# Causal mask of single-head score banks: from a matmul into VectorE's row maximum

## What is computed

```python
scores = jnp.einsum('bhqd,bhkd->bhqk', q, k_h) / math.sqrt(HEAD_DIM)
causal = jnp.triu(jnp.ones((t, t), dtype=bool), k=1)
scores = jnp.where(causal[None, None], jnp.finfo(scores.dtype).min, scores)
attn = jax.nn.softmax(scores, axis=-1)
ctx = jnp.einsum('bhqk,bhkd->bhqd', attn, v_h)
return ctx @ Wo
```

## Time and profile before

| | us |
|---|---|
| three runs | 1482.33, 1478.23, 1481.91 |
| median | 1481.91 |
| the profiled execution | 1481.86 |
| its span | 1480.0 |
| TensorE, VectorE busy | 1381.3, 1026.3 |
| ScalarE, GpSimd busy | 729.4, 683.0 |

### The profile page before, as it was taken

How to read it: one execution, slowest core, us unless ns; L and a number is a source line. 1 busy time by engine, 2 the same in 40 slices (tenths; PEclk the granted TensorE clock), 3 DMA queues, 4 the chain that set the end, 5 groups by cost and what they waited for, 6 DMA issues and landing times. The chain is left out here.

```text
span 1480.0 us, 20324 instructions
## 1 busy us (share of the span) xinstructions
PE 1381.3 (93%) x7032; PEld 1085.2 (73%) x7032; DVE 1026.3 (69%) x1934; ACT 729.4 (49%) x1574; POOL 683.0 (46%) x533
## 2 busy tenths in 40 slices
PE   4779999988898699999999999999999999699999
PEld 3656666665676578888888888888888887578887
DVE  6768998785757587777877787777777787532323
ACT  3547887676434355454544444544544445243332
POOL 3448887666352544244333543434424431054543
PEclk9979999999999899999999999999999999899999
DMA  3000000100110211010110110101101010033332
GB/s 106 4 26 1 1 1 1 29 2 15 51 36 1 72 30 43 15 30 29 29 36 9 43 29 16 43 15 29 44 15 29 22 43 1 15 93 94 96 97 80
DMA packets 64933, 50.73 MB, mean 34 GB/s; under 512 B 5760, under 2 KB 54272, under 8 KB 64576
## 3 DMA queue, kind: packets, MB, share of 16 engines
q1 hardware_dynamic: 64832, 49.43, 11.7%
HBM read 47.32 MB, written 2.10 MB: 33 GB/s over the span
## 5 line engine op out<-in xcount | busy, mean ns | idle before, releaser
L1669 POOL TENSOR_TENSOR a_p_lo<-a_prob,a_p_hi 128x512 fp32r<-128x512 f32 x160 | 203.8, 1288 | 89.3 <-ACT a_p_hi L1559 87.2
L682 ACT ACTIVATE a_pt_hi<-a_ring 128x512 fp32r<-128x512 f32 x160 | 93.9, 596 | 172.0 <-PE a_ring L392 171.9
L818 POOL TENSOR_TENSOR a_rot_a<-a_rot_a,a_rot_b 128x512 f32<-128x512 f32 x80 | 103.4, 1293 | 151.1 <-DVE a_rot_b L561 150.3
L673 ACT ACTIVATE a_prob<-a_score,a_nmax 128x128 f32<-128x128 f32 (+3 forms) x256 | 132.2, 530 | 57.8 <-DVE a_nmax L526 57.7
L333 PE MATMUL a_xo<-h_hi,a_w_hi 128*128 128x512 f32 x384 | 154.0, 401 | 5.3 <-POOL a_w_lo L828 4.2
L2282 POOL TENSOR_TENSOR f_w_lo<-raw,f_w_hi 128x512 fp32r<-128x512 f32 (+2 forms) x66 | 90.5, 1395 | 145.2 <-ACT f_w_hi L2225 145.2
L335 PE MATMUL a_xo<-h_hi,a_w_lo 128*128 128x512 f32 x384 | 151.3, 394 | 0.0
L334 PE MATMUL a_xo<-h_lo,a_w_hi 128*128 128x512 f32 x384 | 150.1, 391 | 0.0
L823 POOL TENSOR_TENSOR a_p_lo<-a_rot_a,a_p_hi 128x512 fp32r<-128x512 f32 x80 | 103.6, 1295 | 70.3 <-ACT a_p_hi L699 70.3
L543 DVE TENSOR_TENSOR a_pt_lo<-a_ring,a_pt_hi 128x512 fp32r<-128x512 f32 x160 | 108.5, 686 | 32.6 <-ACT a_pt_hi L682 31.4
L1559 ACT ACTIVATE a_p_hi<-a_prob 128x512 fp32r<-128x512 f32 x160 | 99.7, 630 | 45.5 <-PE a_cbank L1190 43.2
(11 more groups left out here) (327 smaller groups left out, 3784.7 us busy)
## 6 DMA issues: line engine op xcount, KB each, us to landing
raw<-in_L_gate_up_t SPq DMA_DIRECT2D x40, 256.0 KB, 3.0
raw<-in_L_attn_wq SPq DMA_DIRECT2D x32, 256.0 KB, 2.9
raw<-in_L_attn_wo SPq DMA_DIRECT2D x32, 256.0 KB, 2.6
raw<-in_L_down_t SPq DMA_DIRECT2D x20, 256.0 KB, 2.7
x<-in_L_attn_x SPq DMA_DIRECT2D x4, 512.0 KB, 5.5
raw<-in_L_attn_wk SPq DMA_DIRECT2D x8, 256.0 KB, 2.8
raw<-in_L_attn_wv SPq DMA_DIRECT2D x8, 256.0 KB, 2.8
out<-x SPq DMA_DIRECT2D x8, 256.0 KB, 2.5
```

What stands on the lines that cost most here:

```text
L673: nc.scalar.activation(prob[i % 2][:, h, 0:n], score[e % NS][:, (h % per) * n:(h % per + 1) * n], ACT.Exp, bias=nmax[:, i % 2, h:h + 1], a ...
L818: nc.gpsimd.tensor_tensor(rot_a[:, c % 2, :], rot_a[:, c % 2, :], rot_b[:, c % 2, :], ALU.add).then_inc(summed, 1)
L1669: nc.gpsimd.tensor_tensor(p_lo[:, mm % NP, :], prob[:, mm % NE, :], p_hi[:, mm % NP, :].bitcast(F32), ALU.subtract).then_inc(p_ready, 1)
```

## The change

In banks of one head the mask matmul is gone, and the score matmul signals `scored` itself. VectorE reads the bank with `tensor_tensor_reduce`: it adds the bank and `mask_w`, scales by -1, writes that back to the bank (which nobody reads), and gives the minimum, which is the negated maximum of the masked row. Tiles 0 and 1 are as before, and so are the turned scores and the second attention.

```diff
+def masked_maximum(nc, m, bank, n, to):
+
+    scores = bank[:, 0:n]
+    return nc.vector.tensor_tensor_reduce(scores, scores, m.mask_w[:, T - n:T], -1.0, LARGE, ALU.add, ALU.min, to)
...
                 out = claim_score()
+                scored_by[QT * u + i] = count["score"]
+                if per == 1:
+                    nc.tensor.matmul(out[:, 0:n], q_rows[:, bank, :], k_rows[:, u % 2, x, 0:n], start=True,
+                                     stop=True).then_inc(scored, 1)
+                    return
                 for h in range(per):
...
                                  start=False, stop=True).then_inc(scored, 1)
-                scored_by[QT * u + i] = count["score"]
...
                 per, n = HPG // S_BANKS[i], (i + 1) * P
+                if per == 1:
+                    if u == 0 and i == 2:
+                        dve.wait_ge(zeroed, 3)
+                    masked_maximum(nc, m, next_score(), n, nmax[:, i % 2, bank, x:x + 1]).then_inc(score_read, 1)
+                    return
                 nc.vector.tensor_reduce(nmax[:, i % 2, bank * per:(bank + 1) * per, x],
...
+            nc.vector.memset(m.mask_w[:, 0:T - P], 0.0).then_inc(zeroed, 1)
```

```diff
-        rsum, head_sum = sb("rsum", [P, 2, HPG, X2]), sb("head_sum", [P, 2, HPG, X2, HD0])
+        rsum, head_sum = sb("rsum", [P, 2, HPG, X2]), sb("head_sum", [P, HPG, X2, HD0])
...
-                s, r = head_sum[:, n % 2, :, :, :], rsum[:, n % 2, :, :]
+                s, r = head_sum[:, :, :, :], rsum[:, n % 2, :, :]
...
-        m.ident, m.mask = sb("ident", [P, P]), sb("mask", [P, P])
-        m.mask_t = sb("mask_t", [P, P])
-        m.ident_b, m.mask_b, m.mask_t_b = (sb(n, [P, P], BF16) for n in ("ident_b", "mask_b", "mask_t_b"))
-        m.ident_r = sb("ident_r", [P, P], F32R)
+        m.ident, m.mask_w = sb("ident", [P, P]), sb("mask_w", [P, T])
+        m.mask = m.mask_w[:, T - P:T]
+        m.ident_b, m.mask_b = (sb(n, [P, P], BF16) for n in ("ident_b", "mask_b"))
...
+        m.mask_t, m.mask_t_b, m.ident_r = m.mask_w[:, 0:P], fsb("mask_t_b", [P, P], BF16), fsb("ident_r", [P, P], F32R)
```

More of the change, by code:

```diff
@@ L32 @@
 EPS = 1e-5
+LARGE = 3.0e38
 FF_TILES = [(at, min(P, FF - at)) for at in range(0, FF, P)]
@@ L2302, in program @@
         x_out = out.rearrange("b (t p) d -> p (b t) d", p=P)
+        m.h_hi, m.h_lo = sb("h_hi", [P, KT, NT * P], F32R), sb("h_lo", [P, KT, NT * P], F32R)
+        m.raw = sb("raw", [P, NRAW, 512])
+        m.loaded, m.loads_before = [sem(f"loaded{k}") for k in range(NRAW)], [0] * NRAW
+        first_half = ExitStack()
+        fsb = lambda n, shape, dt=F32: first_half.enter_context(nc.sbuf_tensor(n, shape, dt))
+        m.f_hi, m.f_lo = fsb("f_hi", [P, NT * P], F32R), fsb("f_lo", [P, NT * P], F32R)
+        m.w_both = fsb("w_both", [P, 2, 2, FH], F32R)
+        m.b_st = fsb("b_st", [P, FH + D], F32R)
+        m.mask_t, m.mask_t_b, m.ident_r = m.mask_w[:, 0:P], fsb("mask_t_b", [P, P], BF16), fsb("ident_r", [P, P], F32R)
+        m.a_raw, m.pick = fsb("a_raw", [P, KT, 2 * R]), fsb("pick", [P, 2])
         with nc.Block() as block:
@@ L2322, in stage @@
             return scope, lambda n, shape, dt=F32: scope.enter_context(nc.sbuf_tensor(n, shape, dt)), name == phases[0]
[L2324 to L2332, removed]
         def pieces(x, width):
```

## The result

| | before | changed |
|---|---|---|
| median of 20 runs each, us | 1479.88 | 1482.62 |
| range | 1477.11 to 1482.42 | 1479.20 to 1485.95 |
| ratio, 95% interval | | 1.0018 [1.0009, 1.0026] |
| span of the profiled execution | 1480.0 | 1480.7 |
| stage ends (first clearing of `f_a_st` behind it), us | 381.18 | 382.77 |

The kernel became slower by 0.18%. That is inside the 0.3% that I had called the limit of a measurement; with 20 runs on each side the interval excludes 1, so the loss of 2.7 us is real, and the forecast of −2 us has the wrong sign.

A forecast was written before the change was run, and what follows sets the result against it. TensorE was taken as the bound, VectorE close behind. Terms of −0.5 (units 1 to 4 and 7), −0.8 (units 5 and 6) and −0.7 (unit 0) sum to −2.0 us from 1481.86: 1480 us, range 1470 to 1492.

The forecast's parts named there:

- the forecast of −2 us: Whole kernel: the unit terms sum to −2.0 us, giving 1480 us against the profiled 1481.86.
- What bounds the kernel: Middle units of the first attention: TensorE busy 29.3 of 29.57 us looks like the bound, VectorE close behind at 26.6.
- What is removed: TensorE, query tiles 2 and 3: 128 mask matmuls at 0.13 us, 2.1 us per unit, 16.6 us in all.
- What is added: VectorE, same banks: a second instruction per reduction at 0.08 us, 1.3 us per unit, 10.2 us in all.
- The vanished waits: VectorE behind the first fused instruction: waits of 0.7 us for scores and 0.3 for the context can vanish, 1.0 us.
- What it comes to in a middle unit: VectorE's last maximum comes 0.3 us later, largely absorbed by L1370's wait for GpSimd: 0.0 to −0.2 us per unit.
- The other units: Units 5 and 6, with projections, −0.4 us each; unit 0, starting from empty queues, −0.5 to −1 us.
- VectorE becomes the bound: Last three maxima of tile 3 and the wait for `parted`: slower, +3 to +11 us, up to 1499; chance 0.23.
- my rule of 0.09: VectorE's fused banks: the kernel gets slower once the pair costs over 0.09 us more per bank.
- The mask's read: Fused instruction's SBUF read of the mask contends with GpSimd, +0.44 us each, giving 1530 us; chance 0.03.
- The zeroing, the single buffer and the masks' places: 384-column zeroing before the stage, one buffer for head sums, new mask addresses: claimed to cost nothing.

The follow-up runs named there:

- Experiment 9: Kernel before with the maxima split by single-input reductions and the reciprocals of the row sums in PSUM, mask matmul and plain reduction kept: 1472.1 us, ratio 0.9947.
- experiment 2: Changed kernel with the plain reduction back in single-head banks, mask matmuls still removed (TensorE's part alone): 1477.4 us, ratio 0.9985.
- experiment 3: Changed kernel with the mask matmul back, so the mask is added twice (VectorE's part alone): 1487.4 us, ratio 1.0052.
- experiment 1: Changed kernel with mask matmul and plain reduction back in single-head banks, leaving only its memory and zeroing changes: 1480.6 us, ratio 1.0006.
- experiment 5: Kernel before with the maxima split by three single-input reductions: 1479.7 us, ratio 1.0002.
- experiment 4: Changed kernel with the maxima split by three single-input reductions in place of the copy and the subtraction: 1475.7 us, ratio 0.9972.
- experiment 6: Changed kernel with only the copy of the maxima made a one-element reduction, the subtraction kept: 1474.3 us, ratio 0.9974.

## Why the prediction was wrong

- **What bounds the kernel.** I took PE's 29.3 busy of 29.57 us for a bound with VectorE close behind. Experiment 9 does TensorE's same work in 28.65 us. Some 0.6 us of the "busy" time before was work stretched around waits. Wrong, by 0.9 us per unit.
- **What is removed.** 0.13 us per mask, from starts between other matmuls; measured 0.088 where TensorE does not wait, so 11.3 us in all at most and not 16.6.
- **What is added.** 0.08 us forecast, 0.05 measured in a row of pairs and 0.03 over the unit: 0.45 us in unit 4 and not 1.3. Right in kind, and less than I had taken. With it alone the forecast would have been a larger gain.
- **The vanished waits.** 1.0 us forecast, 1.1 measured. Right.
- **What it comes to in a middle unit.** This is the step that failed. I had seen that L1370 waits for GpSimd, and reasoned that one such wait could only absorb lateness, or shrink if a faster TensorE feeds GpSimd earlier: 0.0 to −0.2 us. It did neither. It stayed at 1.19, and a second instruction, the copy L1368 just ahead of it, joined it: +0.85 us in unit 4 (0.17 to 1.02), and the multiplications went from 2.59 to 3.00 us. So unit 4 is 0.43 us longer. The copy had been short because it fell into a gap of GpSimd's. The faster TensorE closes that gap (experiment 2), which is the opposite of what I had expected of it, and without the faster TensorE the pairs alone make the copy miss it (experiment 3). My sum has no term for the copy and none for the gap; for both the trace of the kernel before has the numbers (0.42 us of idle time, and the copy at 0.17 that starts in it).
- **The other units.** −0.35 and −0.4 for units 5 and 6, −0.5 for unit 0: as forecast, or within 0.2 us. For units 5 and 6 that is partly luck: eight masks at 0.088 are 0.7 us and not 1.0, eight pairs at 0.03 to 0.05 are 0.2 to 0.4 and not 0.6, and the two errors cancel. In units 1 to 4 the forecast was about −0.4 together, and they came out at +0.9, +0.5, +2.1 and +0.4. The last unit with its tail is 1.5 us shorter (72.4 to 70.9), which I had at −0.1; the granted clock there is 0.98 in the one profile and 0.95 in the other, so not all of it is the change. The stage starts 0.4 later; together +1.6 at its end.
- **The rivals.** "VectorE becomes the bound" was the right place (last maxima of tile 3, the wait for `parted`), with another cause than the pair's price: at 0.05 us it would not have decided by my rule of 0.09. The mask's read does not meet GpSimd: the fused instruction takes 712 ns on average, the plain reduction 682. The zeroing, the single buffer and the masks' places cost nothing (experiment 1).

## What to carry to other kernels

Where VectorE and GpSimd work side by side, list VectorE's copies between SBUF tensors and its instructions with two SBUF inputs, tiny ones too: each can take as long as one GpSimd instruction (1.29 us here). Whether it does depends on GpSimd's gaps, which a speed-up elsewhere can close and a delay of 0.1 us can miss. Cure them all together (a reduction for a copy, a PSUM operand for one of two SBUF inputs), since curing one can move the wait to the next (experiment 5); with none cured, 0.1 of 7.0 us saved on TensorE arrived here, with one 4.5, with both 5.6. And do not read a busy share of 99% as a bound while a wait at the unit's end is in the list: take the waits away and look again.

## What was unexpected of the hardware

- A copy of 128x8 elements from SBUF to SBUF lasted until the GpSimd instruction that was running had ended, 0.92 to 1.23 us where that one was in its first 0.4 us, and 0.17 to 0.19 where GpSimd was idle or within 0.16 us of its end; the reductions in its place took 0.17 at most in all 96 cases of experiment 4, and in all 32 of experiment 6.
- The accumulator read of a fused VectorE instruction shows 139 ns, but the next instruction of its kind starts together with it: the pair adds 0.05 us to a row of reductions, and 0.03 on average over a unit.
- Writing a bank back to PSUM costs VectorE nothing over writing one column: the fused instruction lasts 0.68 us where it stands first, as the plain reduction does.
